# A two-layer recurrent kernel on one core: weight tiles of 64 columns in place of 32, and h streamed as 32 columns in place of 16

## What is computed

```python
xW = einsum('ntd,dg->ntg', x, Wx) + b          # x: (2, 1024, 256), Wx: (256, 1024)
def step(carry, xw_t):
    prev_h, prev_c = carry
    a = xw_t + prev_h @ Wh                     # Wh: (256, 1024)
    i = sigmoid(a[:, :256]); f = sigmoid(a[:, 256:512])
    o = sigmoid(a[:, 512:768]); g = tanh(a[:, 768:])
    next_c = f * prev_c + i * g
    next_h = o * tanh(next_c)
...
x = x + lstm(x, cond)                          # h starts from cond
ys = cond / 16
d = rsqrt((ys * ys) @ (weight * weight) + 1e-8)
x = x + ((x * ys) @ weight) * d
```

## Time and profile before

| | |
|---|---|
| median of 3 runs | 1813.32 us (1812.85 to 1816.63) |
| the profiled execution: its own time | 1813.1 us |
| its span, first to last instruction | 1811.3 us |
| PE busy | 1703.1 us (94%) |
| PEld busy | 1642.5 us (91%) |
| DVE, ACT, POOL busy | 1050.7, 1131.1, 259.4 us (58%, 62%, 14%) |
| matmul records, weight-load records | 164,620 each |

### The profile page before, as it was taken

One profiled execution on the slowest core, in us unless ns is written; L12 is line 12 of the kernel. 1 busy time (PEld: TensorE's weight loads), 2 busy tenths in 40 slices (PEclk: granted clock), 3 DMA queues, 4 the chain that ended last, 5 costly groups with the idle time before them and its releaser, 6 DMA issues.

```text
span 1811.3 us, 356718 instructions
## 1 busy us (share of the span) xinstructions
PE 1703.1 (94%) x164620; PEld 1642.5 (91%) x164620; DVE 1050.7 (58%) x7455; ACT 1131.1 (62%) x8196; POOL 259.4 (14%) x1293
## 2 busy tenths in 40 slices
PE   7999999999999999999999999999999999999998
PEld 6999999999999999999999999999999999999996
DVE  3555555555555555555555555555555555555554
ACT  3666666666666666666666666666666666666664
POOL 0111111111111111111111111111111111111110
PEclk8999999999999999999999999999999999999999
DMA  2000000000000000000000000000000000000001
GB/s 95 6 0 0 0 0 0 0 0 0 0 0 0 0 0 0 0 0 0 0 0 0 0 0 0 0 0 0 0 0 0 0 0 0 0 0 0 0 0 46
DMA packets 4585, 6.69 MB, mean 4 GB/s; under 512 B 1248, under 2 KB 3040, under 8 KB 4576
## 3 DMA queue, kind: packets, MB, share of 16 engines
q1 hardware_dynamic: 3872, 5.51, 0.9%
q10 hardware_dynamic: 704, 1.05, 0.2%
HBM read 4.46 MB, written 2.10 MB: 4 GB/s over the span
## 4 chain that ended last, share of the span: by engine, by line
PE 83%; DVE 12%; ACT 3%; issue 2%; DVEq 0%
PE pG L227 31%; PE pX L209 18%; PE pH L227 16%; PE pS L227 13%; DVE parts L370 5%; DVE pH L375 4%; PE pF L240 4%; ACT fgate L185 3%; DVE hst L380 2%; DVE pG L348 1%; PE pG L313 1%; PE pS L304 0%; DVE ores L399 0%; PE pG L236 0%; DVE pH L352 0%
## 5 line engine op out<-in xcount | busy, mean ns | idle before, releaser
L227 PE MATMUL pG<-hst,wh_sb 128*32 128x16 f32 x65536 | 1095.7, 186 | 93.2 <-DVE hst L380 92.3
L227 PEld LDWEIGHTS pG<-hst,wh_sb 128*32 128x32 f32 x65536 | 949.2, 110 | 144.0 <-DVE hst L380 117.1
L227 PE MATMUL pH<-hst,wh_sb 128*32 128x16 f32 x32768 | 762.3, 188 | 3.7 <-issue 3.7
L185 ACT ACTIVATE fgate<-pH 128x2 f32<-128x2 f32 x2048 | 353.9, 173 | 655.2 <-PE pH L227 603.7
L370 DVE TENSOR_TENSOR parts<-fgate,pH 128x2 f32<-128x2 f32 x2048 | 321.5, 157 | 582.5 <-ACT fgate L185 567.1
L227 PEld LDWEIGHTS pH<-hst,wh_sb 128*32 128x32 f32 x32768 | 610.8, 109 | 3.9 <-issue 3.9
L227 PE MATMUL pS<-hst,wh_sb 128*32 128x16 f32 x32768 | 506.6, 186 | 3.4 <-issue 3.4
L209 PE MATMUL pX<-xp,wx_sb 128*32 128x8 f32 x32896 | 459.3, 181 | 1.8 <-issue 1.8
L227 PEld LDWEIGHTS pS<-hst,wh_sb 128*32 128x32 f32 x32768 | 424.3, 108 | 3.6 <-issue 3.6
L146 POOL TENSOR_TENSOR xh<-xh,hst 128x4 f32 (+1 forms) x1024 | 208.5, 204 | 1522.6 <-DVE hst L380 1522.6
L375 DVE TENSOR_TENSOR_SCAN pH<-parts 128x6 f32<-128x6 f32 x2048 | 367.0, 179 | 62.3
(11 more groups left out here) (38 smaller groups left out, 41.3 us busy)
## 6 DMA issues: line engine op xcount, KB each, us to landing
outT_dram<-ores SPq DMA_DIRECT2D x8, 256.0 KB, 2.5
xh<-in_xT_dram SPq DMA_DIRECT2D x6, 320.0 KB, 4.9
wh_sb<-in_Wh_dram ACTq DMA_DIRECT2D x1, 1024.0 KB, 7.8
wx_sb<-in_Wx_dram SPq DMA_DIRECT2D x1, 1024.0 KB, 7.3
w_sb<-in_w_dram SPq DMA_DIRECT2D x1, 256.0 KB, 6.6
xh<-in_xT_dram SPq DMA_DIRECT2D x2, 64.0 KB, 7.9
condT<-in_condT_dram ACTq DMA_DIRECT2D x1, 2.0 KB, 7.6
bias_col<-in_bC_dram ACTq DMA_DIRECT2D x1, 3.0 KB, 7.3
```

Source lines behind the costliest of these rows:

```text
L185: act.activation(fgate[:, j, :], forgets[j][:, cols], ACT.Sigmoid).then_inc(fgate_ready[j], 1)
L227: last = pe.matmul(to[c * Q:(c + 1) * Q, :], tile(wh_sb[:, k, :], c, j, g), hst[:, k, WIDE * t:WIDE * (t + 1)], start=False, stop=True, sk ...
```

## The change

The number of column tiles becomes a constant of its own, NQ = 2 in place of the G = 4 that was also the number of gates, so Q = 128 / NQ is 64. Each call of `sum_x` and `add_h` issues two matmuls of 64 weight columns in place of four of 32. WIDE goes from 16 to 32: `hst` gets windows of 32 columns, two of them h and 30 zeros, and the windows in pG, pH and pS grow with them. The carries still write 8 columns. `clear` and `filler` go through Q as well: two matmuls for each cleared bank, of twice the columns, and a filler with a 64-column weight tile that streams 128 columns as before. The order of calls, the waits, and what ScalarE, VectorE, POOL and the queues do stay as they are.

```diff
     G = 4
-    Q = P // G
+    NQ = 2
+    Q = P // NQ
...
-    WIDE = 16
+    WIDE = 32
...
             def sum_x(to, j, g, k):
-                for c in range(G):
+                for c in range(NQ):
                     last = pe.matmul(to[c * Q:(c + 1) * Q, :], tile(wx_sb[:, k, :], c, j, g), xp[:, k, :],
                                      start=(k == 0), stop=(k == K - 1), skip_group_check=True)
...
-            def add_h(to, t, j, g, k, cs=range(G)):
+            def add_h(to, t, j, g, k, cs=range(NQ)):
                 for c in cs:
                     last = pe.matmul(to[c * Q:(c + 1) * Q, :], tile(wh_sb[:, k, :], c, j, g),
                                      hst[:, k, WIDE * t:WIDE * (t + 1)], start=False, stop=True, skip_group_check=True)
...
-            def cell(t, j, n, k, cs=range(G)):
+            def cell(t, j, n, k, cs=range(NQ)):
...
             def clear(of):
-                for c in range(G):
+                for c in range(NQ):
```

## The result

The changed kernel takes 2,589.2 us (median of 4 runs, 2,589.1 to 2,596.7) against 1,813.5 us before (median of 4): a ratio of 1.4283 (95% interval 1.4252 to 1.4313). The forecast was 2,591. The profiled execution itself took 2,596.7 us, its span is 2,594.9; it is the longest of the four, with a mean granted clock of 0.996 where the other three have 0.999, and in its trace the clock is at 0.50 from 14 to 30 us.

What follows compares the result with a forecast made beforehand. PE's work and a dependence loop both took 1.72 us per step. With dearer 64-column loads, 1,813.1 us plus 777 for 256 bodies plus 1 gave 2,591 us, range 2,390 to 2,720.

Steps and rivals of the forecast that it cites:

- the loop: Dependences from PE's forget sums through ScalarE and VectorE back to PE: 1.72 us per step before the change.
- Loads, not records: PE's time goes by weight columns loaded per tile: a 64-column load 58 ns, a call from about 62 to 116 ns.
- s = 0 and 1: Two of the four steps in a body, each 16 h calls and 6 x calls at 116 ns: 2.55 us each.
- s = 2: Step with 16 h calls, 4 x calls and the filler's two matmuls: 2.54 us.
- s = 3: Step without x sums, where the dependences show: 1.62 us of calls plus 0.67 us back to PE, 2.29 us.
- call 14: Fourteenth of 16 h calls in the step without x sums, at 1.62 us; the first output gate was to wait for it.
- my 0.25 us: Time from the last matmul before the first output gate to ScalarE: 0.19 us of matmul and 0.06 to the gate.
- PE's idle time in s = 3: PE standing idle ahead of pG in the step without x sums, expected at 0.4 us.
- My 0.43: PE's idle time in us within the 2.29 us step without x sums.
- The forget gate's wait: ScalarE's forget gate waiting for PE's sums: to grow from 604 to about 1,400 us.
- A body: Four steps of the kernel: from 6.90 to 9.94 us, 3.04 more each, 777 us over all 256 bodies.
- rival: Other outcomes: faster, 1,731 us, chance 0.09; tiles taking turns, 4,900 us, 0.04; compiler splitting tiles, no change, 1,813 us, 0.02.

Runs made afterwards that it cites:

- The longer stream alone: Kernel before the change, four tiles of 32 kept, with h streamed as 32 columns in place of 16: 1,826.7 us, ratio 1.0064.
- tile-only run: Changed kernel with h streamed as 16 columns again, keeping the two 64-column tiles: 4,573.4 us, ratio 2.5194.
- run with mixed widths: Changed kernel with the x calls back on four tiles of 32 columns, h on two of 64: 2,566.8 us.

## Why the prediction was right, point by point

- **What bounds the kernel before: right.** The longer stream alone adds 12 to 13 us, which fits the longer latency of one matmul in each of 1,024 steps and leaves the loop the bound.
- **Loads, not records: right.** A call of 116 ns was forecast from loads of 32 and 128 columns; 115 to 117 were measured, with half the records. The line through two widths held at the third.
- **s = 0 and 1: right.** 2.57 us against 2.55, PE never idle. The filler and 20 calls of s = 2 together with s = 3 take 1008.06 - 1003.24 = 4.82 us, against 2.54 + 2.29 = 4.83.
- **s = 3: right in its sum, off in its parts.** I had the first output gate wait for call 14. The chain shows it held a step earlier: the cell gate of half 1 waits for call 12, at 1007.41, and the tanh and the output gate follow it without a gap, to 1007.65. Call 14 alone would have let the gate go at about 1007.61 (eight records from 1007.13 at 0.029 us, the last one's 0.22 and the 0.06 to ScalarE), so both paths nearly meet there. And I let a matmul's latency grow by 15 ns, for the stream alone; its record grew by 37, of which 13 go with the stream and 24 with the wider tile, which I had left out. Starting my 0.25 us at the end of call 14, when its last matmul starts before that, made up for it.
- **PE's idle time in s = 3: too high.** I expected 0.4 us ahead of pG, and the profile has 0.24. My 0.43 is counted from where a further call could have started, the profile's idle time from the modelled end of the last matmul. The output gate's last matmul ends at 1007.82 by that model; it started 0.22 earlier, and 0.03 after that start is 1007.63, 0.43 us before the next step's first.
- **The forget gate's wait: too high.** I expected about 1,400 us there, and it is 1,189. ScalarE also stands idle for 126.5 us ahead of its cell gates and 64.2 ahead of its output gates (0.4 and 4.2 before), which would bring the sum to 1,380; but the page puts only 2.0 and 1.7 of that down to PE.
- **The total is nearer than its parts, and that is luck.** A body takes 9.97 us in the profiled execution where I had 9.94, some 8 us more in 256. The 47 us that the kernel before spends outside its bodies (1,813 less 1,766) I carried over with 1 us added; the changed kernel, at its median of 2,589, has about 37 left (with the same body). The two errors nearly cancel. The kernel before loses time at its start: from 22 to 26 us PE is busy for 1.89 of 4.00 us at a clock of 0.50 (the row above the table of loads). Why the changed one loses less outside its bodies stays open.
- **What the sum took for granted.** Every duration in it is one at the full clock, and no rival had another. It came out because the change brings 32 streamed columns with its wider tiles; nothing in the forecast asked whether that was enough for the clock, so here too it was lucky. For the tiles alone the same sum gives 2,585 us, and the chip took 4,573: the step would have failed that multiplies full-clock durations into a kernel whose PE does something else. That PE was to stay busy was no safeguard, since in the tile-only run it is busy for all but 18 us of the span at a clock of 0.50. The Trainium skill, TensorE: Matmul & The Clock Gate, section Why this matters for your kernels, asks that no long idle gap of PE stand between matmul bursts, so that the clock doesn't fall; here the tile-only run has hardly a gap (PE busy for 4,553.9 us of 4,572), and the measurement decides.

## What to carry to other kernels

When each matmul brings new weights, ask how many columns one column tile loads for it: narrow tiles side by side load in parallel, and halving their number nearly doubles a call, however few instructions are left. Here a load's price at a missing width could be read from two others in the same trace. Before the durations of a trace are used in a sum, ask whether the changed PE work will still be granted the clock at which they were taken, and that isn't answered by PE being busy.

## What the runs showed that was not expected

- With two tiles of 64 columns and a stream of 16, PE was busy for 4,553.9 of 4,572 us and stayed at half the clock; with a stream of 32 it had the full clock.
- With four tiles a stream of 8 columns kept the clock at 0.993; with one tile a stream of 64 did not (0.502), and one of 128 did (0.999).
- In the run with mixed widths, a change of tile width between two batches of matmuls cost about 0.12 us each time.
- The record of a matmul grew from 186 to 223 ns, 13 with the stream and 24 with the wider tile, and not further with a stream of 64 in place of 32 columns (224).
